# Causal mask of an attention kernel: from mask matmuls before the exponential to GpSimd selects behind it

## The chip, the cores and the metric

One core of a Trainium2 chip. The metric is the device time in microseconds (us) of one execution, the median of several. The profile is of a single execution. Engines: PE (TensorE, matrix products), DVE (VectorE), ACT (ScalarE), POOL (GpSimd), and SP (SyncE), which here only starts DMA transfers. PSUM is the accumulator memory of PE, of 8 banks; SBUF is the working memory.

## What is computed

The kernel computes attention and a gated feed-forward on the same normalised input, for 4 batches of 512 tokens and width 512, 16 heads of 32, hidden width 1408:

```
xn = layernorm(x)
q, k, v = split(xn @ w_qkv)            # 16 heads of 32
q, k = rope(rmsnorm(q)), rope(rmsnorm(k))
scores = q @ k.T / sqrt(32)
scores = where(q_idx >= k_idx, scores, -1e30)
s = (softmax(scores) @ v) @ w_out
g = silu(down(silu(gate(xn)) * up(xn)))
out = x + s * g
```

The mask lets a query see the keys up to its own position.

## The kernel before, in words

Every engine runs a program of its own, written out by hand, and waits on counting semaphores. Values are split into a high and a low part (`_h`, `_l` or `ph`, `pl`), two reduced-precision numbers whose sum is the full one, and products are taken of both.

**Beats.** `run_beats` steps through 73 beats, c = -8 to 64. Beat j works on head j of 64 (4 batches x 4 groups x 4 heads) and at the same time on later heads: PE projects for beat j + 7, POOL and DVE normalise and rotate for j + 6, PE turns q and k for j + 5 (`turn`), and the row maxima of the group after next are found (`maxima`, `max_turn`) and sent by SP into a spare row of `qst` (`m0_out`, `m_out`). Into the gaps PE puts the gate and up products (`gate_half`, 12 of each 16 beats; the other four turn the next batch's input, `xn_turn`) and the output projection (`out_proj`). The order on each engine is that of its `beat` function. After beat 64 comes the down projection (`down`), whose weights and inputs SP starts to load in beat 57 (`LOAD_AT`), 22 transfers in a row.

**A head.** Of the transposed scores (keys down, queries across) only blocks on and below the causal diagonal are computed, in three groups (`ST_OPS`): widths 512; 384 and 128; 256. Each of the four key blocks begins with a 128 x 128 block on the diagonal. `scores_t(r, c, e)` computes group e. In a key block the diagonal part is masked by a second product into the same bank, identity (`idb`) times a table with -1e30 for keys later than the query (`msk_t`), both bf16. `exps` on ACT takes the exponential twice, as f32 `pf` and as reduced `ph`; `p_low` on DVE makes `pl` = `pf` - `ph` and counts `pl_ok`; `p_v(r, c, e)` on PE waits for `pl_ok` and adds `ph` and `pl` times the values. In beat j PE runs the groups 0, 1, 2 of `scores_t`, and `p_v` of group 0 last; groups 1 and 2 of `p_v` follow in beat j + 1, behind groups 0 and 1 of its scores. `exps` of a group waits for `p_v` of the same group of the head before (`pv_ok`).

**POOL** does, in a beat: `inv_rms` (a `pow` of 8 numbers per partition), `rope` (three products), in some beats `rstd_block`, then `out_sum` (where c mod 4 is 1) and `norm` (where it is 2), for a group of four heads that is done. `norm` waits for `rdb`, the reciprocal row sums, which go through DRAM by two DMAs of SP.

Of the kernel before, what the change touches and what calls it, by code (L numbers as in the profile page):

```python
# [7 lines left out]
ALU = mybir.AluOpType  # L8
# [3 lines left out]
F32R = mybir.dt.float32r  # L12
# [3 lines left out]
B, N, H = 4, 512, 512  # L16
# [31 lines left out]
AT_CG, AT_QST, AT_MX = 129152 // 4, 146016 // 4, 195424 // 4  # L48
# [25 lines left out]
def build(nc, x, w_qkv, w_out, q_gamma, k_gamma, w_gu, s_gate, s_up, w_down, s_down,  # L74
          cos_tab, sin_tab, ident, ident_b, mask_s, mask_t, s_dram, rd_dram, wg_dram, hf_dram, out):
    top = ExitStack()
    with top:
# [39 lines left out]
        msk_t = sb("msk_t", [P, P], BF16)  # L117
# [25 lines left out]
        ph = sb("ph", [P, sum(ST_W)], F32R)  # L143
        pl = sb("pl", [P, sum(ST_W)], F32R)
# [48 lines left out]
        st_full, p_ok, pl_ok, pv_ok, o_ev = (sem(n) for n in ("st_full", "p_ok", "pl_ok", "pv_ok", "o_ev"))  # L193
# [87 lines left out]
        def _(sp):  # L281
# [8 lines left out]
            for dst, src in ((ctab, cos_tab), (stab, sin_tab), (gam[:, 0, :], q_gamma.to_broadcast([P, HD])),  # L290
                             (gam[:, 1, :], k_gamma.to_broadcast([P, HD])), (idb[:], ident_b),
                             (msk_s[:], mask_s), (msk_t[:], mask_t)):
                sp.dma_start(dst, src).then_inc(c_in, 16)
# [192 lines left out]
        def _(pool):  # L486
# [7 lines left out]
            def tables():  # L494

                pool.wait_ge(c_in, 16 * 7)
# [34 lines left out]

            def out_sum(i):

                wait(pool, og_in, 16 * 2 * HG * (i + 1))
                wait(pool, onl_ok, i)
                pool.tensor_tensor(on[:], oh[:], ol[:], ALU.add).then_inc(os_ok, 1)
# [6 lines left out]
            def beat(r, c):  # L543
                j, k = 16 * r + c, c % 4
                if there(j + 6, NB):
                    inv_rms(j + 6, (c + 6) % 2)
                if there(j + 6, NB):
                    rope(j + 6, (c + 6) % 2, (c + 6) % 4)
                b, t = ln_at(r, c)
# [6 lines left out]
                if k == 2 and there(4 * r + (c - 6) // 4, B * G):  # L556
                    norm(4 * r + (c - 6) // 4)

# [420 lines left out]
        def _(pe):  # L979
# [46 lines left out]
            def scores_t(r, c, e):  # L1026
# [7 lines left out]
                for j, c0, w in ST_OPS[e]:  # L1034
                    pe.matmul(bank[:, c0:c0 + w], kst[0:KS + 1, par, h, j * P:(j + 1) * P],  # L1035
                              qst[0:KS + 1, par, h, j * P:N], start=True, stop=False)
                    op = pe.matmul(bank[:, c0:c0 + P], idb[:], msk_t[:], start=False, stop=True)  # L1037
                op.then_inc(st_full, 1)

            def p_v(r, c, e):  # L1040

                j_, v, h = 16 * r + c, c // 4 % VR, c % 4
                pe.wait_ge(pl_ok, NOP * j_ + e + 1)
# [91 lines left out]
            def beat(r, c):  # L1135
# [3 lines left out]
                if isinstance(r, int) and r == 0 and c == -4:  # L1139
                    pe.wait_ge(c_in, 16 * 7)  # L1140
# [155 lines left out]
```

## Time and profile before

| | |
|---|---|
| median of 3 runs | 802.47 us (801.33 to 804.57) |
| profiled execution, its own time | 800.7 us |
| its span, first to last instruction | 798.7 us |
| mean granted TensorE clock | 0.967 |
| PE, DVE, ACT, POOL busy | 716.4, 536.0, 450.0, 291.9 us |

The busy times are sums over the span. The end of a PE row is modelled, so the busy share of PE overstates what it does; the distance between starts is the surer measure. A wait in the trace is idle time of an engine that ended when another's result came.

### The profile page before, as it was taken

The numbers are of one execution on the slowest core, as the hardware profiler recorded it, in microseconds if no ns is written. First come the engines' busy times: TensorE is split into PE (matmuls) and PEld (weight loads), VectorE is DVE, ScalarE is ACT, GpSimd is POOL, SyncE is SP. The second block draws the span as 40 slices with busy tenths as digits, with TensorE's granted clock in tenths as the row PEclk, the third lists the DMA queues.
The fourth block names the chain that finished last, engine by engine and source line by source line (L and its number), as shares of the span: only waits on it lengthen the run. The fifth ranks groups of instructions, "written<-read, shape, count | busy, mean of one in ns | idle before, by whom it ended". The sixth has DMA issues, their size and how long they took to land.

```text
span 798.7 us, 12896 instructions
## 1 busy us (share of the span) xinstructions
PE 716.4 (90%) x4160; PEld 575.3 (72%) x4160; DVE 536.0 (67%) x1051; ACT 450.0 (56%) x1007; POOL 291.9 (37%) x338
## 2 busy tenths in 40 slices
PE   2589999889999999899999999899999972798997
PEld 2477877777787887677878877778788751586885
DVE  2677677887767677867676677776764672746373
ACT  1444666577565555766665567766655672634230
POOL 5544335555444434553433445534333330100000
PEclk9699999999999999999999999999999995699999
DMA  8154433412333332123333222033332136278672
GB/s 289 32 170 153 147 127 116 135 54 75 93 106 94 114 103 71 54 68 95 105 94 121 87 74 67 15 94 107 94 118 87 50 117 223 73 253 298 211 251 92
DMA packets 59280, 94.36 MB, mean 118 GB/s; under 512 B 12752, under 2 KB 15440, under 8 KB 59216
## 3 DMA queue, kind: packets, MB, share of 16 engines
q1 hardware_dynamic: 59216, 93.56, 36.9%
q8 instruction: 34, 0.56, 0.3%
q14 instruction: 30, 0.25, 0.1%
HBM read 59.06 MB, written 25.82 MB: 106 GB/s over the span
## 4 chain that ended last, share of the span: by engine, by line
PE 73%; DVE 8%; issue 5%; DMA 5%; SPq 3%; POOL 2%; ACT 2%; DVEq 0%; ACTq 0%; POOLq 0%
PE bank L1115 19%; PE bank L1010 17%; PE bank L1051 8%; PE bank L1131 6%; PE bank L1091 5%; PE bank L1035 5%; PE bank L1072 5%; PE bank L1022 3%; PE bank L1037 2%; PE bank L1074 2%; DVE pl L821 2%; SPq L346 1%; DVE qn L798 1%; DMA rd_dram<-rd 1%; DVE mx L840 1%
## 5 line engine op out<-in xcount | busy, mean ns | idle before, releaser
L840 DVE TENSOR_REDUCE mx<-bank 128x1 f32<-128x384 f32 (+3 forms) x176 | 109.4, 636 | 88.0 <-PE bank L1074 87.2
L517 POOL TENSOR_TENSOR rr<-ss,half 128x8 f32<-128x8 f32 x64 | 106.3, 1661 | 149.1 <-DVE ss L791 149.1
L625 ACT ACTIVATE pf<-bank 128x512 f32<-128x512 f32 (+1 forms) x192 | 101.0, 526 | 101.5 <-PE bank L1037 68.9
L821 DVE TENSOR_TENSOR pl<-pf,ph 128x512 fp32r<-128x512 f32 (+1 forms) x192 | 132.0, 688 | 15.6 <-ACT ph L626 15.1
L523 POOL TENSOR_TENSOR ra<-qn,cg 128x256 f32<-128x256 f32 x64 | 47.0, 734 | 153.3 <-DVE qn L798 153.3
L1115 PE MATMUL bank<-xnt_h,wgu 128*128 128x512 f32 x352 | 98.7, 402 | 3.7 <-DVE g L867 1.6
L626 ACT ACTIVATE ph<-bank 128x512 fp32r<-128x512 f32 (+1 forms) x192 | 101.2, 527 | 0.0
L1115 PE MATMUL bank<-xnt_l,wgu 128*128 128x512 f32 x352 | 96.3, 395 | 0.0
L1035 PE MATMUL bank<-qst,kst 97*128 97x512 f32 (+3 forms) x256 | 81.8, 373 | 13.9 <-DMA qst<-mrow 13.5
L1072 PE MATMUL bank<-kst,qst 96*128 96x128 f32 (+3 forms) x256 | 83.7, 378 | 1.3 <-DVE mx L840 1.3
L1051 PE MATMUL bank<-ph,va 128*65 128x512 f32 (+3 forms) x256 | 76.9, 326 | 4.9 <-ACT oraw L634 3.0
L526 POOL TENSOR_TENSOR rb<-qn,sg 128x128 f32<-128x128 f32 x128 | 79.4, 640 | 0.0
L1115 PEld LDWEIGHTS bank<-xnt_l,wgu 128*128 128x128 f32 x352 | 66.1, 188 | 16.3
L1010 PE MATMUL bank<-wq_h,xnt_h 128*128 128x384 f32 x256 | 62.0, 365 | 17.3 <-DVE va L802 15.7
L614 ACT ACTIVATE kst<-bank 96x512 fp32r<-96x512 f32 x64 | 38.1, 595 | 60.5 <-PE bank L1022 59.5
L1010 PE MATMUL bank<-wq_h,xnt_l 128*128 128x384 f32 x256 | 72.0, 365 | 0.0
L1051 PE MATMUL bank<-pl,va 128*65 128x512 f32 (+3 forms) x256 | 71.9, 317 | 0.0
L1131 PE MATMUL bank<-wd,ht_h 128*128 128x512 f32 x176 | 70.7, 402 | 1.2 <-DVE wd L883 0.8
L1115 PEld LDWEIGHTS bank<-xnt_h,wgu 128*128 128x128 f32 x352 | 60.8, 188 | 14.5 <-issue 4.9
L1131 PE MATMUL bank<-wd,ht_l 128*128 128x512 f32 x176 | 70.3, 400 | 0.0
L1035 PEld LDWEIGHTS bank<-qst,kst 97*128 97x128 f32 x256 | 51.3, 200 | 22.0 <-DMA qst<-mrow 14.3
L1022 PE MATMUL bank<-idr,tt 128*96 128x128 f32 x512 | 55.7, 232 | 10.0 <-DVE xnt_l L785 6.0
(84 smaller groups left out, 1400.6 us busy)
## 6 DMA issues: line engine op xcount, KB each, us to landing
wgu<-wg_dram SPq DMA_DIRECT2D x66, 256.0 KB, 2.8
hf_dram<-g SPq DMA_DIRECT2D x44, 256.0 KB, 3.0
hf_raw<-hf_dram SPq DMA_DIRECT2D x44, 256.0 KB, 6.0
wg_dram<-wgu SPq DMA_DIRECT2D x22, 256.0 KB, 3.1
xr<-x SPq DMA_DIRECT2D x16, 256.0 KB, 3.4
stage<-w_gu SPq DMA_DIRECT2D x16, 256.0 KB, 3.4
oh<-oraw SPq DMA_DIRECT2D x64, 64.0 KB, 1.9
ol<-oraw SPq DMA_DIRECT2D x64, 64.0 KB, 2.0
```

Source lines behind the costliest of these rows:

```text
L517: pool.tensor_tensor(rr[:, s, :], ss[:, s, :], half[:], ALU.pow).then_inc(rr_ok, 1)
L625: act.activation(pf[:, tile], bank[:, 0:w], ACT.Exp, scale=SCALE)
L626: act.activation(ph[:, tile], bank[:, 0:w], ACT.Exp, scale=SCALE).then_inc(p_ok, 1)
L821: dve.tensor_tensor(pl[:, tile], pf[:, tile], ph[:, tile].bitcast(F32), ALU.subtract).then_inc(pl_ok, 1)
L840: dve.tensor_reduce(mx[:].rearrange("p (h t) -> p h t", t=TB)[:, h0:h0 + len(heads), qb], bank[:, 0:len(heads) * w].rearrange("p (h n) -> ...
L1010: op = pe.matmul(QKV_PS[:, 0:3 * GC], x_[:, k, t * P:(t + 1) * P], w_[:, k, cols], start=(a == 0), stop=(a == len(todo) - 1))
L1022: op = pe.transpose(W_PS[0:KS, h * P:(h + 1) * P].bitcast(F32R), tt[:, s, h, 3 * a:3 * a + 3, :].rearrange("p c d -> p (c d)"), idr[:])
L1035: pe.matmul(bank[:, c0:c0 + w], kst[0:KS + 1, par, h, j * P:(j + 1) * P], qst[0:KS + 1, par, h, j * P:N], start=True, stop=False)
L1051: op = pe.matmul(PV_PS[0:VW, j * P:N], va[:, v, j, h, :], part[:, a:a + w], start=(j == 0 and part is ph), stop=(j == 2 and part is pl))
L1072: pe.matmul(bank[:, a * w:(a + 1) * w], qst[0:KS, par, h, qb * P:(qb + 1) * P], kst[0:KS, par, h, 0:w], start=True, stop=False)
L1115: op = pe.matmul(GU_PS[:], wgu[:, s, k, :], x_[:, k, :], start=(a == 0), stop=(a == len(todo) - 1))
L1131: op = pe.matmul(DN_PS[t][:], h_[:, m, t * P:(t + 1) * P], wd[:, m, :], start=(m == 0 and h_ is ht_h[b % 2]), stop=(m == MT - 1 and h_ is ...
```

## The change

The table `msk_t`, its load and the second product of `scores_t` go, so the exponentials above the diagonal are taken of unmasked scores. `ph` and `pl` become halves of one tile `pp`. A new POOL function `keep_past(j, e)` waits for `pl_ok` of the group and, for each of its key blocks, writes zero over the entries above the diagonal in both halves at once (an `affine_select` of 128 partitions x 2 x 128), then counts `tri_ok`. `p_v` waits for `tri_ok` in the place of `pl_ok`. Loads counted by `c_in` are one fewer.

```
-        ph = sb("ph", [P, sum(ST_W)], F32R)
-        pl = sb("pl", [P, sum(ST_W)], F32R)
+        pp = sb("pp", [P, 2, sum(ST_W)], F32R)
+        ph, pl = pp[:, 0], pp[:, 1]
...
+            def keep_past(j, e):
+
+                pool.wait_ge(pl_ok, NOP * j + e + 1)
+                for _, c0, _ in ST_OPS[e]:
+                    a = ST_AT[e] + c0
+                    op = pool.affine_select(pp[:, :, a:a + P], pp[:, :, a:a + P], [[0, 2], [1, P]], ALU.is_ge, 0.0,
+                                            base=0, channel_multiplier=-1)
+                op.then_inc(tri_ok, 1)
...
                     inv_rms(j + 6, (c + 6) % 2)
+                if there(j, NB):
+                    keep_past(j, 0)
                 if there(j + 6, NB):
                     rope(j + 6, (c + 6) % 2, (c + 6) % 4)
+                if there(j, NB):
+                    keep_past(j, 1)
                 b, t = ln_at(r, c)
...
                     norm(4 * r + (c - 6) // 4)
+                if there(j, NB):
+                    keep_past(j, 2)
...
                 for j, c0, w in ST_OPS[e]:
-                    pe.matmul(bank[:, c0:c0 + w], kst[0:KS + 1, par, h, j * P:(j + 1) * P],
-                              qst[0:KS + 1, par, h, j * P:N], start=True, stop=False)
-                    op = pe.matmul(bank[:, c0:c0 + P], idb[:], msk_t[:], start=False, stop=True)
+                    op = pe.matmul(bank[:, c0:c0 + w], kst[0:KS + 1, par, h, j * P:(j + 1) * P],
+                                   qst[0:KS + 1, par, h, j * P:N], start=True, stop=True)
...
-                pe.wait_ge(pl_ok, NOP * j_ + e + 1)
+                pe.wait_ge(tri_ok, NOP * j_ + e + 1)
```

On PE, the first rows of a beat in the middle of the program, before: two groups of scores (L1035, with the mask products L1037), a product for the maxima (L1072) and the first of `p_v` (L1051).

```order
L1035 MATMUL bank<-qst,kst 128x512 [waits p_ok]
L1037 MATMUL bank<-msk_t,idb 128x128
L1035 MATMUL bank<-qst,kst 128x384 [waits p_ok]
L1037 MATMUL bank<-msk_t,idb 128x128
L1035 MATMUL bank<-qst,kst 128x128
L1037 MATMUL bank<-msk_t,idb 128x128
L1072 MATMUL bank<-kst,qst 128x384 [waits sm_ok,tk_ev,tq_ev]
L1074 MATMUL bank<-msk_s,idb 128x128
L1051 MATMUL bank<-ph,va 65x384 [waits pl_ok]
L1051 MATMUL bank<-pl,va 65x384
L1051 MATMUL bank<-ph,va 65x128
L1051 MATMUL bank<-pl,va 65x128
```

The same place in the changed kernel (line numbers shift: L1049 is `scores_t`, L1085 `maxima`, L1064 `p_v`):

```order
L1049 MATMUL bank<-qst,kst 128x512 [waits p_ok]
L1049 MATMUL bank<-qst,kst 128x384 [waits p_ok]
L1049 MATMUL bank<-qst,kst 128x128
L1085 MATMUL bank<-kst,qst 128x384 [waits sm_ok,tk_ev,tq_ev]
L1087 MATMUL bank<-msk_s,idb 128x128
L1064 MATMUL bank<-pp,va 65x384 [waits tri_ok]
L1064 MATMUL bank<-pp,va 65x384
L1064 MATMUL bank<-pp,va 65x128 x2
```

The three mask products are gone, weights of one scores product now follow those of another directly, and `p_v` waits for `tri_ok`.

On POOL, the rows of one beat with `norm` before (`inv_rms` L517, `rope` L523 and L526, `norm` L541), and the first of the next beat:

```order
L517 TENSOR_TENSOR rr<-ss,half 128x8 [waits ss_ok]
L523 TENSOR_TENSOR ra<-qn,cg 128x256 [waits qp_ok,qn_ok]
L526 TENSOR_TENSOR rb<-qn,sg 128x8x16 x2
L541 TENSOR_TENSOR on<-on,rdb 128x512 [waits rb_in,os_ok]
L517 TENSOR_TENSOR rr<-ss,half 128x8 [waits ss_ok]
```

The same beat in the changed kernel (`inv_rms` L516, `rope` L522 and L525, `norm` L549, the selects L536):

```order
L516 TENSOR_TENSOR rr<-ss,half 128x8 [waits ss_ok]
L536 AFFINE_SELECT pp<-pp 128x2x128 [waits pl_ok]
L522 TENSOR_TENSOR ra<-qn,cg 128x256 [waits qp_ok,qn_ok]
L525 TENSOR_TENSOR rb<-qn,sg 128x8x16 x2
L536 AFFINE_SELECT pp<-pp 128x2x128 [waits pl_ok]
L536 AFFINE_SELECT pp<-pp 128x2x128
L549 TENSOR_TENSOR on<-on,rdb 128x512 [waits rb_in,os_ok]
L536 AFFINE_SELECT pp<-pp 128x2x128 [waits pl_ok]
L516 TENSOR_TENSOR rr<-ss,half 128x8 [waits ss_ok]
```

One select now stands ahead of `rope`, two ahead of `norm`, and the last behind `norm`, so it can't start before `norm` has had its DMA.

## Rows read from the trace of the kernel before

**Rows 1.** The page's chain that ended last: shares of the span by engine

```profile
PE 73%; DVE 8%; issue 5%; DMA 5%; SPq 3%; POOL 2%; ACT 2%; DVEq 0%; ACTq 0%; POOLq 0%
```

**Rows 2.** Windows: length, busy us (count) of PE, PEld, DVE, ACT, POOL; PE clock, DMA

```profile
100.00:630.00 530.00, 508.06 (x3131) 410.08 (x3131) 378.12 (x761) 332.31 (x770) 232.43 (x249) 1.00 0.30 90
```

**Rows 3.** PE's waits, 100 to 630, then 600 to 700: total us, times, longest

```profile
PE bank L1010 <- DVE va L802: 12.5, 21, 1.0
PE bank L1022 <- DVE xnt_l L785: 2.2, 9, 0.3
...
PE bank L1035 <- DMA qst<-mrow: 13.5, 1, 13.5
```

**Rows 4.** Timeline of PE: start us, duration us, line, out<-in, form, count

```profile
612.77 0.28 PE L1035 MATMUL bank<-qst,kst 97*128 97x256 f32 x1
...
612.94 1.17 PE L1091 MATMUL bank<-wo_h,on_l 128*128 128x512 f32 x4
613.95 0.86 PE L1010 MATMUL bank<-wq_h,xnt_h 128*128 128x384 f32 x4
...
619.38 0.39 PE L1051 MATMUL bank<-pl,va 128*65 128x512 f32 x1
619.61 0.39 PE L1035 MATMUL bank<-qst,kst 97*128 97x512 f32 x1
...
619.88 0.42 PE L1035 MATMUL bank<-qst,kst 97*128 97x384 f32 x1
...
620.18 0.30 PE L1035 MATMUL bank<-qst,kst 97*128 97x128 f32 x1
...
620.37 0.47 PE L1072 MATMUL bank<-kst,qst 96*128 96x512 f32 x1
...
622.27 0.33 PE L1051 MATMUL bank<-pl,va 128*65 128x384 f32 x1
622.44 0.22 PE L1051 MATMUL bank<-ph,va 128*65 128x128 f32 x1
...
622.56 0.28 PE L1051 MATMUL bank<-ph,va 128*65 128x256 f32 x1
622.68 0.28 PE L1051 MATMUL bank<-pl,va 128*65 128x256 f32 x1
```

**Rows 5.** POOL's instructions by form: count | busy us, mean ns | idle before

```profile
L517 POOL TENSOR_TENSOR rr<-ss,half 128x8 f32<-128x8 f32 x64 | 106.3, 1661 | 149.1 <-DVE ss L791 149.1
...
L523 POOL TENSOR_TENSOR ra<-qn,cg 128x256 f32<-128x256 f32 x64 | 47.0, 734 | 153.3 <-DVE qn L798 153.3
...
L505 POOL TENSOR_SCALAR hsc<-sgu 128x11 f32<-128x11 f32 x1 | 0.3, 255 | 5.8 <-DMA sgu<-s_up 5.8
```

**Rows 6.** Timeline of DVE, POOL and PE in one steady beat

```profile
404.81 0.68 DVE L821 TENSOR_TENSOR pl<-pf,ph 128x512 fp32r<-128x512 f32 x1
...
407.81 1.29 POOL L541 TENSOR_TENSOR on<-on,rdb 128x512 f32<-128x512 f32 x1 [0.33 <-DMA rdb<-rd_dram]
...
407.95 1.70 DVE L821 TENSOR_TENSOR pl<-pf,ph 128x512 fp32r<-128x512 f32 x1
...
411.44 0.41 DVE L821 TENSOR_TENSOR pl<-pf,ph 128x256 fp32r<-128x256 f32 x1
...
414.87 0.29 PE L1051 MATMUL bank<-ph,va 128*65 128x256 f32 x1
```

**Rows 7.** Timeline of POOL and PE where `norm` comes late

```profile
335.55 1.28 POOL L541 TENSOR_TENSOR on<-on,rdb 128x512 f32<-128x512 f32 x1 [2.71 <-DMA rdb<-rd_dram]
...
337.01 0.28 PE L1051 MATMUL bank<-ph,va 128*65 128x256 f32 x1
...
688.66 0.42 PE L1051 MATMUL bank<-ph,va 128*65 128x256 f32 x1
...
690.94 1.28 POOL L541 TENSOR_TENSOR on<-on,rdb 128x512 f32<-128x512 f32 x1 [9.45 <-DMA rdb<-rd_dram]
...
694.03 0.77 PE L1131 MATMUL bank<-wd,ht_h 128*128 128x512 f32 x1 [0.79 <-DVE wd L883]
```

More of the change, by code:

```diff
@@ L47 @@
 RING = 4
-AT_CG, AT_QST, AT_MX = 129152 // 4, 146016 // 4, 195424 // 4
+AT_CG, AT_QST, AT_MX = 128896 // 4, 145760 // 4, 195168 // 4
 HELD_B = AT_CG - 65536 // 4 - MT * N
@@ L74, in build @@
 def build(nc, x, w_qkv, w_out, q_gamma, k_gamma, w_gu, s_gate, s_up, w_down, s_down,
-          cos_tab, sin_tab, ident, ident_b, mask_s, mask_t, s_dram, rd_dram, wg_dram, hf_dram, out):
+          cos_tab, sin_tab, ident, ident_b, mask_s, s_dram, rd_dram, wg_dram, hf_dram, out):
     top = ExitStack()
@@ L116, in build @@
         msk_s = sb("msk_s", [P, P], BF16)
-        msk_t = sb("msk_t", [P, P], BF16)
         gam = sb("gam", [P, 2, HD])
@@ L192, in build @@
         m0_in = sem("m0_in")
-        st_full, p_ok, pl_ok, pv_ok, o_ev = (sem(n) for n in ("st_full", "p_ok", "pl_ok", "pv_ok", "o_ev"))
+        st_full, p_ok, pl_ok, tri_ok, pv_ok, o_ev = (sem(n) for n in ("st_full", "p_ok", "pl_ok", "tri_ok", "pv_ok", "o_ev"))
         og_in, d_in, rd_ok, rd_out, rb_in = (sem(n) for n in ("og_in", "d_in", "rd_ok", "rd_out", "rb_in"))
@@ L291, in _ @@
                              (gam[:, 1, :], k_gamma.to_broadcast([P, HD])), (idb[:], ident_b),
-                             (msk_s[:], mask_s), (msk_t[:], mask_t)):
+                             (msk_s[:], mask_s)):
                 sp.dma_start(dst, src).then_inc(c_in, 16)
@@ L494, in tables @@
             def tables():
-                pool.wait_ge(c_in, 16 * 7)
+                pool.wait_ge(c_in, 16 * 6)
                 for a in range(2):
@@ L1139, in beat @@
                 if isinstance(r, int) and r == 0 and c == -4:
-                    pe.wait_ge(c_in, 16 * 7)
+                    pe.wait_ge(c_in, 16 * 6)
                     pe.wait_ge(ones_ok, 4)
@@ L1280 @@
         "mask_s": np.where(tri[None, :] > tri[:, None], NEG, 0.0).astype(ml_dtypes.bfloat16),
-        "mask_t": np.where(tri[:, None] > tri[None, :], NEG, 0.0).astype(ml_dtypes.bfloat16),
     }
@@ L1292 @@
           d["s_up"], d["w_down"], d["s_down"], d["cos_tab"], d["sin_tab"], d["ident"], d["ident_b"],
-          d["mask_s"], d["mask_t"], s_dram, rd_dram, wg_dram, hf_dram, out)
+          d["mask_s"], s_dram, rd_dram, wg_dram, hf_dram, out)
     r = run_bass_kernel_spmd(nc, [arrays], core_ids=[0])
```

## The prediction

> **What bounds the kernel now.** I read four things in turn. The chain that ended last [rows 1]: 73% of it is TensorE (PE). Then the steady stretch, 100 to 630 us [rows 2]: PE busy 508 of 530 us at full granted clock, VectorE (DVE) 378, GpSimd (POOL) 232. The stretch holds 53 beats (53 `ra` groups on POOL, one for each), so a beat is 10.0 us, with 9.6 us of PE, 7.1 us of DVE and 4.4 us of POOL. Then what PE waits for there [rows 3]: mostly DVE's evacuation of the projection bank, 12.5 us in 21 waits, and the low part of the turned input, 2.2 us in 9. So PE's instruction stream is the bound, and what is taken from it comes off the time, except in the beats with such a wait. Last the end: one wait of 13.5 us for a DMA of the row maxima [rows 3]. That DMA stands in SP's queue behind the 22 loads that SP issues at `LOAD_AT` (beat 57), so what happens in beats 57 to 59 vanishes in that wait, for good or ill.
>
> **What the removed matmuls cost.** Four a beat, 256 in all. A PE row ends by a model, so I go by the distance from start to start [rows 4]. For the first two groups of a beat, with masks: 619.61 to 619.88 is 0.27 us (512 columns and a mask), to 620.18 another 0.30 (384 and a mask), to 620.37 another 0.19 (128 and a mask): 0.76 us. Without a mask the same widths take 0.23 us (512, 619.38 to 619.61), 0.17 (384, 622.27 to 622.44) and 0.06 (128, 622.44 to 622.56 is two of them): 0.46. Saved: 0.30 us. The mask itself shows only 0.04 us from its start to the next; the rest is the next weight load, which a short mask matmul can't cover and a wide one can. For the third group, 256 columns and a mask take 0.17 us (612.77 to 612.94) against 0.12 (622.56 to 622.68), and the four 512-column matmuls behind it take 1.01 us (612.94 to 613.95) against 4 x 0.23 = 0.92 with nothing exposed. Saved: 0.05 + 0.08, that is 0.13. **In all 0.42 us a beat.** The low end is 0.04 x 4 = 0.16, if the weight loads stay exposed for another reason.
>
> Beats 0 to 56 count: 57 x 0.42 = 23.9 us. In the 21 beats that wait for the projection bank, the third group stands between DVE's source and that wait, so its 0.13 us only lengthens the wait: 21 x 0.13 = 2.7 off. The first two groups lie ahead of the PE result on which DVE then waits, and stay saved. That leaves 21.2 us.
>
> **What the selects cost.** Four `affine_select` a beat, each 128 partitions x 256 f32 elements (the high and the low half of one 128-column block), one input. The trace has none. The nearest rows [rows 5]: 734 ns for a two-input product of the same size; 255 ns for a one-input operation of 11 elements, a floor, as it is nearly all start-up. The `pow` at 1661 ns for 8 elements warns that an operation with software of its own can cost far more than its size says; I keep it as the upper end. I take 0.5 us, midway between floor and product, since one input is read and the comparison is simple. Four are 2.0 us, and POOL comes to 6.4 us of a beat of 9.6.
>
> The Trainium skill (GPSIMD Engine Reference, section 4.1 on engine selection) tells to keep elementwise work off GpSimd, where two inputs halve the rate while one input runs near line rate; no select is in this trace to check that on.
>
> **Where the selects lie.** `keep_past(j, 0)` runs between `inv_rms` and `rope`, in the time in which POOL waits for `qn`. The low part that it waits for ends at 404.81 + 0.68 = 405.49 in [rows 6]; its reader `p_v(j, 0)` is the last thing in PE's beat, behind two gate halves and the projection. It is hidden. `keep_past(j, 1)` (two selects) waits for a low part that ended at 409.65, and its reader comes in the next beat just ahead of 414.87: hidden too. `keep_past(j, 2)` follows a low part that ends at 411.85; the reader is the row at 414.87, 3.0 us later, some 2.7 with the masks gone. With 0.5 us it is hidden, if POOL is free. What gives way behind it is `inv_rms`, which fits, since its input is ready only about then.
>
> Two costs remain. First the lock. In [rows 6] a low-part subtraction (two SBUF inputs) that takes 0.68 us took 1.70, because POOL's product had started 0.14 us before it: it ended 0.55 us after POOL did, so it did nothing until then. The skill (SBUF — State Buffer, section on who interferes with whom) says just this: an exclusive lock between a DVE operation with two SBUF inputs and a GpSimd operation that reads SBUF. The trace agrees: 1.02 us lost to a 1.29 us product. So each select can hold DVE's `p_low`, `t_low` and `rope_sum` for up to 0.5 us; if all four did so in every beat, DVE would come to 7.1 + 2.0 = 9.1 us of 9.6, the second rival's case. In ordinary beats DVE has 2.9 us idle and PE waits for it nowhere, so this is free. In the four beats a batch that turn the next batch's input there are no gate matmuls ahead, and PE waits on DVE twice (all 9 waits for the input's low part [rows 3], and my count puts most of the 21 there too): a hold there comes straight through. I price it at two holds of 0.5 us a batch, three batches: 3 us.
>
> Second POOL's own queue. `keep_past(j, 2)` stands behind `norm`, which waits for the `rdb` DMA. Where the gate matmuls fill the beats, `norm` is early: 407.81 + 1.29 = 409.10 against 414.87 [rows 6]. Once a batch, where they are missing, it is not: 335.55 + 1.28 = 336.83 against 337.01 [rows 7]. There PE stalls 0.5 to 1 us, but in these same beats it later waits on DVE for about as much, and that chain starts ahead of the stall; I count 0.5 us for all. At the end it is worse: `norm` of group 14 starts at 690.94 after a long wait, and the third group of head 62 now stands behind it, which PE reached at 688.66 [rows 7]. Its select ends near 692.7, then head 63's last scores, exponentials, low part and select have to follow, and the last weight conversions on DVE behind those, which the down projection at 694.03 waits for. I put that at 2.5 us. The same thing at head 58 falls into the 13.5 us wait.
>
> Sum: 21.2 - 3 - 0.5 - 2.5 = 15.2 us saved; the freed constant DMA at the start is under half a microsecond and left out. Against the profiled execution's own 800.7 us this is 785.5. The median of the runs is 1.8 us above that execution, so the forecast is **787.5 us**, 1.9% faster.
>
> **Rivals.**
> *The masks were nearly free.* The weight loads stay exposed and only the 0.16 us a beat is saved: 57 x 0.16 = 9.1, less 4 to 6 for the costs above: about 798. For it: the model of PE's ends. Against: the start distances are not modelled ends, and all three distances that begin right behind a mask (0.30, 0.19 and the 1.01 of four) hold the same 0.09 more than their columns need. Chance 0.08.
> *DVE is held everywhere.* If the selects delay DVE's chain to the projection bank in ordinary beats too, by the 0.4 us that PE saved, the gain goes into those waits: 57 x 0.42 given back, about 800. Against: only 21 of the 53 beats wait for it now, and of DVE's two-input operations only `t_low` and `p_low(j, 0)` stand ahead of it in a beat, with one select at most beside each. Chance 0.10.
> *Slower: POOL becomes the bound.* POOL has 10.0 - 4.4 = 5.6 us free in a beat of today, so from 1.4 us a select it sets the pace. At the 1.66 us of `pow` a beat takes 4.4 + 6.6 = 11.0 us, 1.0 more than now: 57 us, about 860. For it: POOL's software operations are the least predictable rows here. Against: 256 elements through one input should not cost twice the two-input product. Between 1.0 and 1.4 us latencies pile up (`rope` late, DVE held 4 us a beat) and the time is somewhere between 800 and 810. Chance 0.13 for all of it.
> My forecast (780 to 794) holds 0.69.
>
> **How the numbers follow.** A measurement here tells about 0.5% (4 us) from no change. Faster by more than that: the forecast, the first rival's better half and a part of the second, 0.78. Within 0.5%: 0.09. Slower: 0.13. The range runs from 779 (all 23.9 us saved, nothing paid) to 801 (the second rival); what is left out is the slower case and a little at the bottom.
>
> **What would show it.** In the changed kernel's profile: the start distance from the first to the third scores matmul of a beat down from 0.57 to about 0.40; a select near 0.5 us; POOL busy about 130 us more; 256 fewer matmuls on PE; the waits on DVE's projection evacuation longer by about 0.13 each, not more frequent; new waits of PE on a select in few beats, the longest at heads 58 and 62. The forecast is wrong if a select is over 1 us, if PE waits for selects in ordinary beats, or if the 512-wide low-part subtractions grow to well above 1 us on average and PE's waits on DVE multiply.

## The result, and the profile after

The changed kernel takes 795.62 us (median of 11 runs, 792.33 to 802.14) against 802.47 (11 runs, 800.48 to 804.7): the ratio is 0.9926 with a 95% interval of 0.9899 to 0.9954. It is faster, by 0.7%, where 1.9% was forecast. By the medians 6.9 us are gained, less than half of the 15.2 us forecast. The profiled execution took 794.34 us, its span is 792.2 us. Against the forecast of 787.5 us, 8.1 us of gain are missing.

The page's chain that ended last, shares of the span by engine, and part of its shares by line, answers to [rows 1]:

```profile
PE 63%; DMA 10%; POOL 8%; DVE 7%; issue 6%; SPq 4%; ACT 1%; DVEq 0%; POOLq 0%; ACTq 0%
PE bank L1128 18%; PE bank L1024 15%; PE bank L1064 6%; PE bank L1144 6%; PE bank L1104 5%; PE bank L1085 4%; DMA rdb<-rd_dram 3%; PE bank L1049 3%; PE bank L1036 3%; DMA rd_dram<-rd 2%; POOL rr L516 2%; PE bank L1087 2%; SPq L345 1%; POOL pp L536 1%; DVE pp L835 1%
```

PE gave up ten points of the chain (73 to 63). POOL took six of them, but DMA took five, and the DMAs named are not the big loads: they are `rd_dram<-rd` and `rdb<-rd_dram`, the way of the softmax reciprocals through DRAM to `norm`. That is the first pointer to the cause.

PE's waits over the whole span (total us, times, longest), of which [rows 3] shows the stretches for before:

```profile
PE bank L1064 <- POOL pp L536: 19.3, 11, 4.8
PE bank L1024 <- DVE va L816: 17.7, 25, 2.0
PE bank L1049 <- DMA qst<-mrow: 9.3, 1, 9.3
PE bank L1036 <- DVE xnt_l L799: 6.0, 8, 1.6
```

Then two rows of the page's costliest groups: the select, which no earlier row priced (x instructions, busy us, mean ns, idle before), and DVE's low part:

```profile
L536 POOL TENSOR_SCALAR_AFFINE_SELECT pp<-pp 128x256 fp32r<-128x256 f32 x256 | 109.5, 440 | 159.2 <-DVE pp L835 159.2
...
L835 DVE TENSOR_TENSOR pp<-pf,pp 128x512 fp32r<-128x512 f32 (+1 forms) x192 | 127.1, 663 | 15.2 <-ACT pp L640 14.4
```

A select takes 0.44 us, and the low part did not get longer on average (688 ns before, 663 now). That mean mixes two forms: taken apart, the low part of 512 columns fell from 813 to 697 ns and that of 256 columns rose from 436 to 594, so selects do hold DVE, but elsewhere less is held. The price of a select is not the miss; what the lock has to do with it comes below. The 19.3 us of waits on a select fall in 11 places: the longest are 2.8 us between the first scores of heads 27 and 28 and, in the last beats, 4.8 and 3.9.

**Where along the run.** I took the start of the first 512-column scores matmul of each head from PE's timeline, and from those starts the length of each beat, in both kernels. Over heads 0 to 57 the time fell from 570.6 to 558.2 us, so 12.4, where the sum had 17.7 (21.2 less 3 and 0.5). In 48 of these 57 beats the difference is even: -0.40 us on average, 19.3 us in all. The missing part sits in the other nine, those that end at heads 7, 8, 11, 12, 27, 28, 43, 44 and 45: together they are 6.9 us **longer** than before, and one of them, from head 27 to 28, has 2.9 of it.

These are rows of that beat and of the one before it, on POOL, PE, DVE and SP's queue, in the changed kernel (start us, duration us, what it is; in brackets the idle time before it and what ended it):

```profile
319.29 0.24 DVE L861 RECIPROCAL rd<-den 128x16 f32<-128x16 f32 x1
320.07 0.95 POOL L536 TENSOR_SCALAR_AFFINE_SELECT pp<-pp 128x256 fp32r<-128x256 f32 x2
320.98 1.46 POOL L544 TENSOR_TENSOR on<-oh,ol 128x512 f32<-128x512 f32 x1
322.51 0.53 SPq L355 DMA_DIRECT2D oh<-oraw  x1
323.73 0.57 SPq L367 DMA_DIRECT2D rd_dram<-rd  x1
326.89 0.60 SPq L375 DMA_DIRECT2D rdb<-rd_dram  x1
330.51 0.66 PE L1064 MATMUL bank<-pp,va 128*65 128x384 f32 x4
332.31 1.26 POOL L549 TENSOR_TENSOR on<-on,rdb 128x512 f32<-128x512 f32 x1 [4.43 <-DMA rdb<-rd_dram]
333.53 0.41 POOL L536 TENSOR_SCALAR_AFFINE_SELECT pp<-pp 128x256 fp32r<-128x256 f32 x1
333.90 1.64 POOL L516 TENSOR_TENSOR rr<-ss,half 128x8 f32<-128x8 f32 x1
333.99 0.45 PE L1064 MATMUL bank<-pp,va 128*65 128x256 f32 x2 [2.82 <-POOL pp L536]
336.74 1.62 PE L1024 MATMUL bank<-wq_h,xnt_h 128*128 128x384 f32 x4 [0.24 <-DVE va L816]
```

Read it from the top. The two selects of group 1 stand ahead of `out_sum` (L544). It ends at 322.44. The reciprocals have been ready since 319.53, but in SP's queue their store stands behind the next group's gathers into `oh` and `ol`, which may not overwrite what `out_sum` still reads: so `out_sum` releases the gathers (322.51), and behind them the reciprocals go out (323.73) and back (326.89). `norm` (L549) starts at 332.31, after POOL has waited 4.43 us. PE had ended group 1's `p_v` at 331.17 and waits 2.82 us for a select of 0.41 us that stands behind `norm`. The next row of PE that matters, the projection at 336.74, takes 1.62 us for four matmuls that take 0.94 at 318.32 in the same trace. The windows say why (length, busy us and count of PE, PEld, DVE, ACT, POOL, then the granted clock):

```profile
330.00:335.00 5.00, 2.04 (x13) 1.23 (x12) 1.99 (x5) 2.88 (x6) 2.69 (x3) 1.00 0.09 33
335.00:340.00 5.00, 4.24 (x18) 3.57 (x19) 3.20 (x7) 1.21 (x4) 3.66 (x7) 0.51 0.11 28
340.00:345.00 5.00, 4.94 (x30) 4.19 (x30) 2.46 (x7) 3.44 (x10) 2.05 (x2) 0.81 0.11 30
```

PE is busy 2.04 of 5 us around the stall, and right after it the granted clock is 0.51, which is the lower of the two levels, 1.2 GHz. So the stall is paid for a second time. But the kernel before has a low clock in this beat too, with the same row:

```profile
340.38 1.62 PE L1010 MATMUL bank<-wq_h,xnt_h 128*128 128x384 f32 x4 [0.49 <-DVE va L802]
```

From there to the first scores of head 28 it takes 4.83 us (340.38 to 345.21) and the changed kernel 5.68 (336.74 to 342.42). Of the 2.9 us between the two kernels in this beat, about 0.85 are therefore the longer stretch at the low clock, and the rest is mainly the stall itself.

### The profile page after: what moved, and what is told of

Same layout as the page of the kernel before. It is cut to its first block, busy times and chain, and to the rows that moved or that the text cites. A ratio compares the mean times of both kernels' runs of the same rounds, so it can differ in the third digit from the quotient of the medians.

```text
span 792.2 us, 12640 instructions
## 1 busy us (share of the span) xinstructions
PE 699.1 (88%) x3904; PEld 576.4 (73%) x3904; DVE 537.5 (68%) x1051; ACT 449.3 (57%) x1007; POOL 399.8 (50%) x594
## 4 chain that ended last, share of the span: by engine, by line
PE 63%; DMA 10%; POOL 8%; DVE 7%; issue 6%; SPq 4%; ACT 1%; DVEq 0%; POOLq 0%; ACTq 0%
PE bank L1128 18%; PE bank L1024 15%; PE bank L1064 6%; PE bank L1144 6%; PE bank L1104 5%; PE bank L1085 4%; DMA rdb<-rd_dram 3%; PE bank L1049 3%; PE bank L1036 3%; DMA rd_dram<-rd 2%; POOL rr L516 2%; PE bank L1087 2%; SPq L345 1%; POOL pp L536 1%; DVE pp L835 1%
## 5 line engine op out<-in xcount | busy, mean ns | idle before, releaser
L536 POOL TENSOR_SCALAR_AFFINE_SELECT pp<-pp 128x256 fp32r<-128x256 f32 x256 | 109.5, 440 | 159.2 <-DVE pp L835 159.2
L835 DVE TENSOR_TENSOR pp<-pf,pp 128x512 fp32r<-128x512 f32 (+1 forms) x192 | 127.1, 663 | 15.2 <-ACT pp L640 14.4
L516 POOL TENSOR_TENSOR rr<-ss,half 128x8 f32<-128x8 f32 x64 | 107.5, 1680 | 53.6 <-DVE ss L805 53.6
L1064 PE MATMUL bank<-pp,va 128*65 128x512 f32 (+3 forms) x512 | 105.9, 328 | 22.7 <-POOL pp L536 19.3
L640 ACT ACTIVATE pp<-bank 128x512 fp32r<-128x512 f32 (+1 forms) x192 | 100.9, 526 | 0.0
L1064 PEld LDWEIGHTS bank<-pp,va 128*65 128x65 f32 x512 | 59.0, 144 | 39.5 <-POOL pp L536 23.6
L1085 PE MATMUL bank<-kst,qst 96*128 96x128 f32 (+3 forms) x256 | 82.7, 375 | 0.0
L1024 PE MATMUL bank<-wq_h,xnt_h 128*128 128x384 f32 x256 | 60.9, 362 | 19.3 <-DVE va L816 17.7
L1049 PE MATMUL bank<-qst,kst 97*128 97x512 f32 (+3 forms) x256 | 68.1, 341 | 9.3 <-DMA qst<-mrow 9.3
L1024 PE MATMUL bank<-wq_h,xnt_l 128*128 128x384 f32 x256 | 74.0, 373 | 0.0
L525 POOL TENSOR_TENSOR rb<-qn,sg 128x128 f32<-128x128 f32 x128 | 72.7, 588 | 0.0
L1128 PEld LDWEIGHTS bank<-xnt_h,wgu 128*128 128x128 f32 x352 | 61.1, 188 | 11.6 <-issue 2.7
L1049 PEld LDWEIGHTS bank<-qst,kst 97*128 97x128 f32 x256 | 50.5, 201 | 21.9 <-DMA qst<-mrow 10.1
```

The source lines that it names most:

```text
L516: pool.tensor_tensor(rr[:, s, :], ss[:, s, :], half[:], ALU.pow).then_inc(rr_ok, 1)
L536: op = pool.affine_select(pp[:, :, a:a + P], pp[:, :, a:a + P], [[0, 2], [1, P]], ALU.is_ge, 0.0, base=0, channel_multiplier=-1)
L640: act.activation(ph[:, tile], bank[:, 0:w], ACT.Exp, scale=SCALE).then_inc(p_ok, 1)
L835: dve.tensor_tensor(pl[:, tile], pf[:, tile], ph[:, tile].bitcast(F32), ALU.subtract).then_inc(pl_ok, 1)
L1024: op = pe.matmul(QKV_PS[:, 0:3 * GC], x_[:, k, t * P:(t + 1) * P], w_[:, k, cols], start=(a == 0), stop=(a == len(todo) - 1))
L1049: op = pe.matmul(bank[:, c0:c0 + w], kst[0:KS + 1, par, h, j * P:(j + 1) * P], qst[0:KS + 1, par, h, j * P:N], start=True, stop=True)
```

## The experiments

Each ratio is to the kernel before, run beside it on the same chip; it is worked out from all runs of both, so it can differ by 0.1 to 0.3 points from that of the medians. The column "to head 57" is the stretch from head 0 to head 57 in the one execution that was profiled, which need not be the median one (e2's took 788.44 us, e5's 789.27).

| kernel | median us | ratio, 95% interval | to head 57 |
|---|---|---|---|
| before | 801.3 to 803.1 | 1 | 570.6 |
| changed kernel | 795.62 | 0.9926, 0.9899 to 0.9954 | 558.2 |
| e1 select of group 2 first | 796.42 | 0.9916, 0.9882 to 0.9949 | 560.9 |
| e2 no selects | 785.74 | 0.9788, 0.9756 to 0.982 | 551.6 |
| e3 masks and selects | 811.05 | 1.0097, 1.0062 to 1.0131 | 572.9 |
| e4 both moves | 788.52 | 0.9817, 0.9789 to 0.9846 | 553.3 |
| e5 matmul mask for group 2 | 792.11 | 0.9879, 0.9847 to 0.9911 | 554.9 |
| e6 `out_sum` moved alone | 792.77 | 0.9862, 0.9824 to 0.9899 | 556.7 |
| e7 wider selects, on e4 | 793.60 | 0.9889, 0.9854 to 0.9923 | 559.1 |
| e8 group 2's select moved alone | 792.69 | 0.9877, 0.9845 to 0.991 | 555.0 |
| e9 e4, `norm` a beat later | 784.49 | 0.9774, 0.9747 to 0.9802 | 549.6 |
| e10 `norm` a beat later, alone | 784.87 | 0.9788, 0.9759 to 0.9817 | 551.3 |
| e11 before, `norm` a beat later | 800.96 | 0.9976, 0.9956 to 0.9995 | 569.5 |

**First: is it the place in GpSimd's queue, or are selects costly wherever they stand?** The theory (Q) was the queue: `keep_past(j, 2)` behind `norm`. The rival (L) was the lock on DVE and the selects' own latency.

e1 puts the select of group 2 ahead of `out_sum` and `norm`.

```diff
                 b, t = ln_at(r, c)
                 if t is not None:
                     rstd_block(b, t)
...
+                if there(j, NB):
+                    keep_past(j, 2)
                 if k == 1 and there(4 * r + (c - 5) // 4, B * G):
                     out_sum(4 * r + (c - 5) // 4)
                 if k == 2 and there(4 * r + (c - 6) // 4, B * G):
                     norm(4 * r + (c - 6) // 4)
-                if there(j, NB):
-                    keep_past(j, 2)
```

> The third select group of a beat, keep_past(j, 2), stands ahead of out_sum and norm on GpSimd instead of behind them. All else is the changed kernel. Theory Q (queue): what is missing from the forecast was lost because this select waited behind norm, and norm for its DMA. Then TensorE's waits for a select between 100 and 630 us (6.9 us in 5) fall to under 1 us, the lumps of 1 to 3 us at heads 7, 8, 12, 28, 44 and 45 shrink, and the time falls by 6 to 9 us to about 787. Theory L (lock): it was lost because selects hold VectorE's two-input operations. The selects are as many and as long, so the time stays within 2 us of 795.6.

Measured 796.42: no gain, which is the result that theory L was given. Yet in its trace PE waits for no select between 100 and 610 us. What PE waits for there instead:

```profile
PE bank L1024 <- DVE va L816: 17.4, 21, 2.3
PE bank L1036 <- DVE xnt_l L799: 3.9, 9, 0.8
```

Against 12.5 and 2.2 before [rows 3]. Four beats, those that end at heads 8, 11, 12 and 44, are 1.8 to 2.5 us longer than before. In the one from head 11 to 12 `norm` starts 0.11 us ahead of DVE's `t_low` (L829), an operation with two SBUF inputs, which then takes 1.45 us instead of 0.42:

```profile
177.68 1.28 POOL L549 TENSOR_TENSOR on<-on,rdb 128x512 f32<-128x512 f32 x1 [0.96 <-DMA rdb<-rd_dram]
177.79 1.45 DVE L829 TENSOR_TENSOR tt<-qp,tt 128x256 fp32r<-128x256 f32 x1 [0.35 <-ACT tt L616]
```

PE waits 0.63, 0.23 and 0.21 us for DVE behind it, and the granted clock is 0.72 in the window from 180 to 185. One beat earlier `out_sum` (167.91) does the same to `t_low` (168.38, 1.09 us). So the order of POOL's queue also decides which DVE operation `norm` and `out_sum` collide with. The theory, "one select is in the wrong place", was too narrow.

e2 leaves out the selects (and so the causal mask of the diagonal blocks); e3 has the mask matmuls and the selects.

```diff
-                if there(j, NB):
-                    keep_past(j, 0)
...
-                pe.wait_ge(tri_ok, NOP * j_ + e + 1)
+                pe.wait_ge(pl_ok, NOP * j_ + e + 1)
```

> No mask matmuls and no selects: p_v waits for pl_ok, and entries above the diagonal of the diagonal blocks stay in the probabilities (the causal mask is left out there). This is the whole gain of the removed matmuls with no cost of the selects. By the forecast's first term: 57 beats x 0.42 us less the 2.7 us that goes into existing waits, so 21 us below the kernel before, about 781. If the mask matmuls had been worth only their own 0.04 us each, it would be about 794. Both Q and L expect the first; what lies between this run and the changed kernel is what the selects cost.

> The changed kernel with the mask matmuls put back beside the selects, so masked twice: the kernel before plus the selects. Price of the selects at the old pace of TensorE. Q: slower than the kernel before by 5 to 9 us (the late norms of heads 10, 26, 42 and the tail), with the stalls 0.3 to 0.6 us shorter each than in the changed kernel, since the beats are longer. L: also slower by that, but spread over the beats: VectorE's waits grow and each ordinary beat is 0.1 us or more longer.

e2 measured 785.74 where about 781 was expected. To head 57 it saves 19.0 us, a tenth less than the 21.2 forecast; over the whole program it saves 17 us; in its profiled execution the part behind the first down projection is 4.0 us longer than before, which is left open. e3 measured 811.05, 8 us above the kernel before, as expected under Q. By e2 and the changed kernel the selects cost 10 to 11 us, by e3 and the kernel before 8: the loss belongs to the selects, with the masks or without. Theory L expected e3's ordinary beats to be 0.1 us longer each; the 48 even ones differ from the kernel before by 0.02 us on average, and the beats that end at heads 12 and 44 by 2.5 and 1.1.

e4 has both moves: `out_sum` ahead of group 1's selects, the select of group 2 ahead of `norm`.

```diff
+                if k == 1 and there(4 * r + (c - 5) // 4, B * G):
+                    out_sum(4 * r + (c - 5) // 4)
                 if there(j, NB):
                     keep_past(j, 1)
...
-                if k == 1 and there(4 * r + (c - 5) // 4, B * G):
-                    out_sum(4 * r + (c - 5) // 4)
+                if there(j, NB):
+                    keep_past(j, 2)
                 if k == 2 and there(4 * r + (c - 6) // 4, B * G):
                     norm(4 * r + (c - 6) // 4)
-                if there(j, NB):
-                    keep_past(j, 2)
```

> As e1, and out_sum stands ahead of keep_past(j, 1) as well, so that SyncE's gathers and the DMAs of the reciprocal sums behind them start as early as in the kernel before. Q: as e1 or up to 2 us faster, about 786, since norm's DMA lands about 1 us earlier. L: no change from the changed kernel, 795. If e4 is slower than e1, the price is keep_past(j, 1) behind out_sum's own wait for its gathers.

Measured 788.52: 7 us come back with all 256 selects in place. What selects cost wherever they stand can then be little more than the 2.8 us left to e2. L falls for the main part. e4 and e1 differ only in the place of `out_sum`, so in e1 that place alone cost 8 us.

**Second: which of the two moves?** e6 has only the first piece of that diff, e8 only the second.

> Only out_sum moves, ahead of the select of group 1; the select of group 2 stays behind norm. If the loss comes by the chain out_sum, its gather, the reciprocals' way through DRAM, norm, the select of group 2, then a sum that is ready a select earlier (about 0.5 to 1 us) takes that much from each late norm: 792 to 794 us. If only the place of the select of group 2 behind norm counts, nothing changes against the changed kernel: 795 to 797 us.

> Only the select of group 2 moves, to just ahead of norm; out_sum keeps its place between the selects of groups 1 and 2. If the place behind norm is what costs, this is as fast as the kernel with both moves, 788 to 790 us. If out_sum's delay by the select of group 1 counts by itself (it holds back the reciprocals and VectorE), 791 to 793 us.

792.77 and 792.69. Against the changed kernel's 0.9926 the ratios are lower by 0.0064 and 0.0049; together that is 0.0113, and e4, with both, is lower by 0.0109. So both count, and they add up as far as intervals of 0.3 to 0.4 points to either side can tell. For e8 that was the second branch of its expectation; its trace shows what is late when the select no longer is:

```profile
331.28 1.45 POOL L549 TENSOR_TENSOR on<-on,rdb 128x512 f32<-128x512 f32 x1 [3.60 <-DMA rdb<-rd_dram]
332.69 1.63 POOL L516 TENSOR_TENSOR rr<-ss,half 128x8 f32<-128x8 f32 x1
334.36 0.43 DVE L812 TENSOR_TENSOR qn<-bank,rr 128x256 f32<-128x256 f32 x1 [2.76 <-POOL rr L516]
334.70 0.28 DVE L816 TENSOR_TENSOR va<-bank,va 128x128 fp32r<-128x128 f32 x1
335.13 1.62 PE L1024 MATMUL bank<-wq_h,xnt_h 128*128 128x384 f32 x4 [3.41 <-DVE va L816]
```

The wait has moved, not gone: `norm` holds POOL's queue until the DMA lands, behind it now stands the next head's `rr`, DVE waits 2.76 us for that, and PE 3.41 us for DVE. What is wrong is that `norm` is reached before its DMA is in, whatever stands behind it.

e5 gives group 2 its mask by matmul again, so that no select stands behind `norm`, and keeps the other selects (`p_v` of group 2 waits for `pl_ok` again). The edit, against the changed kernel:

```diff
-                    op = pe.matmul(bank[:, c0:c0 + w], kst[0:KS + 1, par, h, j * P:(j + 1) * P],
-                                   qst[0:KS + 1, par, h, j * P:N], start=True, stop=True)
+                    op = pe.matmul(bank[:, c0:c0 + w], kst[0:KS + 1, par, h, j * P:(j + 1) * P],
+                                   qst[0:KS + 1, par, h, j * P:N], start=True, stop=e < 2)
+                    if e == 2:
+                        op = pe.matmul(bank[:, c0:c0 + P], idb[:], msk_t[:], start=False, stop=True)
...
-                if there(j, NB):
-                    keep_past(j, 2)
```

> Group 2 of each head gets its mask from a matmul as before and its p_v waits for VectorE's low part again; groups 0 and 1 keep the selects, and no select stands behind the reciprocal's multiplication. By the theory that the loss of the change is GpSimd's queue (the select of group 2 behind out_sum and norm), this keeps 0.30 us of a beat, about 17 us less 2 that move into waits, and loses nothing in mid-run: 787 to 790 us. By the rival that each select costs VectorE or TensorE something wherever it stands, half of the selects leave about half of the loss: 791 to 795 us.

Measured 792.11, in the range given to the rival (791 to 795) and 2 us above the queue's. The number alone would speak for the rival, by which each select costs something wherever it stands. The trace does not: an ordinary beat is 0.33 us shorter (forecast for the first two groups: 0.30), so its three selects cost nothing there. What stays is `norm`: POOL's waits for its DMA are 49.8 us in 13 over the span (53.1 in 14 in the changed kernel), and the beats that end at heads 12, 44 and 45 are 0.3 to 1.3 us longer than before. The one that ends at head 45 is 1.3 us longer in e2 as well, which has no select. The profiled execution was the fastest of six, so the trace may show too little.

e7 is e4 with selects of 256 columns for three of the four blocks (columns beyond the block's diagonal pass the condition, so the result stays).

```diff
-                for _, c0, _ in ST_OPS[e]:
-                    a = ST_AT[e] + c0
-                    op = pool.affine_select(pp[:, :, a:a + P], pp[:, :, a:a + P], [[0, 2], [1, P]], ALU.is_ge, 0.0,
+                for _, c0, w in ST_OPS[e]:
+                    a, w = ST_AT[e] + c0, min(w, 2 * P)
+                    op = pool.affine_select(pp[:, :, a:a + w], pp[:, :, a:a + w], [[0, 2], [1, w]], ALU.is_ge, 0.0,
```

> The order of the kernel with both moves (out_sum ahead of the select of group 1, the select of group 2 ahead of norm), but three of the four selects of a head take 256 columns instead of 128; the result is the same. Each should take 0.2 to 0.3 us longer, 0.7 us of a beat on GpSimd. If the selects lie in GpSimd's slack, the time stays within 2 us of 788.5. If they hold VectorE, or if p_v waits for them at once, 0.1 to 0.2 us of a beat come back: 795 to 800 us.

Its selects take, by form:

```profile
L536 POOL TENSOR_SCALAR_AFFINE_SELECT pp<-pp 128x512 fp32r<-128x512 f32 x192 | 123.5, 644 | 158.0 <-DVE pp L835 158.0
L536 POOL TENSOR_SCALAR_AFFINE_SELECT pp<-pp 128x256 fp32r<-128x256 f32 x64 | 33.2, 519 | 0.0
```

Twice the elements take 0.20 us more than the 0.44 of the changed kernel. 793.60 is 5 us over e4, between the two branches. In ordinary beats the wider selects cost nothing (-0.3 to -0.48 us against before, as in e4). The difference sits in a few beats; those that end at heads 11 and 27 are 2.2 us longer each. The one from head 26 to 27 shows the lock: three selects, two of them wide, run on POOL from 320.64 to 322.58, and beside them DVE's low part and its `t_low` take 0.83 and 0.85 us, where e4 has 0.62 and 0.64 (0.42 is the usual time of both). `t_low`, e7 and then e4:

```profile
321.99 0.85 DVE L829 TENSOR_TENSOR tt<-qp,tt 128x256 fp32r<-128x256 f32 x1
320.35 0.64 DVE L829 TENSOR_TENSOR tt<-qp,tt 128x256 fp32r<-128x256 f32 x1
```

PE has waits of 0.31, 0.64 and 0.56 us close to each other where e4 has 0.52 and 0.56, and then the granted clock falls. e7 first, then e4, the same window:

```profile
325.00:330.00 5.00, 4.81 (x21) 4.20 (x22) 3.23 (x7) 1.28 (x5) 3.35 (x7) 0.66 0.27 79
```

```profile
325.00:330.00 5.00, 4.79 (x34) 3.71 (x33) 4.13 (x10) 4.00 (x10) 3.15 (x6) 1.00 0.17 58
```

Both show PE busy 4.8 of 5 us, but e7 gets 21 matmuls through and e4 34. A few tenths of a microsecond of waiting more became over 2 us. So e7 bears out its second branch in mechanism (the selects hold VectorE) and the first in ordinary beats, where nobody waits for what is held.

**Third: the move that takes the DMA off the queue.** e10 changes one place only: `norm` is issued in the following beat, behind group 1's selects. e9 does the same to e4. e11 does it in the kernel before, behind `rope`.

```diff
                 if there(j, NB):
                     keep_past(j, 1)
+                if k == 3 and there(4 * r + (c - 7) // 4, B * G):
+                    norm(4 * r + (c - 7) // 4)
...
-                if k == 2 and there(4 * r + (c - 6) // 4, B * G):
-                    norm(4 * r + (c - 6) // 4)
```

> The changed kernel with that one move alone: norm a beat later; out_sum keeps its place behind the select of group 1. If out_sum's delay costs only through the norm that comes late by it, this one move gives the whole 7 us back: 786 to 790 us. If out_sum's later place costs by itself (it holds VectorE or the select of group 2), 791 to 794 us.

> The kernel with both moves, and norm a beat later (in the beats where k is 3, behind the select of group 1), when the DMA that brings the reciprocals should have landed in every case. If the loss of the change is work queued on GpSimd behind a norm that waits for that DMA (a select of group 2, or the next head's rr and through it VectorE's qn and va), the last of it goes: 785 to 788 us, at the level of the kernel without selects. If what is left between them is VectorE held or the extra wait for the select, nothing moves: 788 to 790 us.

> The kernel before, masks by matmul and no selects, with norm a beat later, behind the rotary products. If the late norms cost only because selects stand in GpSimd's queue, nothing changes: 801 to 803 us. If the next head's rr behind a norm that waits for its DMA cost the kernel before something too, the same move is worth 1 to 4 us here: 798 to 801 us.

e10 measured 784.87, 11 us under the changed kernel and at e2's level, with every select in place; e9 784.49; both lie a little under the ranges expected. e11 measured 800.96, in the range of its second branch. POOL's waits over the span, e10:

```profile
POOL pp L536 <- DVE pp L835: 188.5, 126, 15.8
...
POOL on L549 <- DMA rdb<-rd_dram: 15.7, 1, 15.7
```

and the same line of the changed kernel:

```profile
POOL on L549 <- DMA rdb<-rd_dram: 53.1, 14, 15.2
```

The one wait left is the last `norm`, behind all attention work. The beat from head 27 to 28 in e10, where the changed kernel stalled 2.82 us:

```profile
331.46 0.90 PE L1064 MATMUL bank<-pp,va 128*65 128x384 f32 x6
334.08 0.41 POOL L536 TENSOR_SCALAR_AFFINE_SELECT pp<-pp 128x256 fp32r<-128x256 f32 x1 [1.90 <-DVE pp L835]
337.16 1.45 POOL L549 TENSOR_TENSOR on<-on,rdb 128x512 f32<-128x512 f32 x1
```

All six matmuls of groups 1 and 2 run in one piece, `norm` starts without a wait. `out_sum` is as late as in the changed kernel; in this beat that costs nothing, and here its effect in e6 was that of an earlier DMA. Elsewhere it does cost. In e10's trace the beat from head 7 to 8 is 3.4 us longer than before: DVE waits 2.53 us for a load of gate and up weights, its gate product stands behind that, PE waits 2.04 us for the product, and the granted clock is 0.54 in the window from 145 to 150.

```profile
139.54 0.43 DVE L892 TENSOR_SCALAR wgu<-stage 128x512 fp32r<-128x512 int32 x1 [2.53 <-DMA stage<-w_gu]
```

Such loads stand in SP's queue behind the gathers that `out_sum` releases and behind the store of the reciprocals: two are issued at 133.04 and 134.01, in e9, where `out_sum` stands earlier, at 127.87 and 129.79, and there DVE does not wait and the beat is 1.3 us shorter than before. (The kernel before and the changed kernel have DVE wait 1.64 and 2.10 us for this load.) e9 still gains nothing on e10 that can be told (the intervals overlap): over the 48 even beats it takes 3.2 us more, all in the six that end at heads 14, 18, 30, 34, 46 and 50. Why an early `out_sum` costs there was not followed.

e11 gains 0.24% (0.05 to 0.44%): the late `norm` cost the kernel before something too. Its expectation put that down to the next head's `rr` behind `norm`, and the trace shows another way. `rr` ends at 338.62 and DVE reads it only at 339.63. But `norm` started at 335.55 [rows 7], 0.01 us ahead of `t_low`, which was held (0.43 us in e11):

```profile
335.56 1.56 DVE L815 TENSOR_TENSOR tt<-qp,tt 128x256 fp32r<-128x256 f32 x1 [0.35 <-ACT tt L602]
```

The maxima behind it came late, PE waited 0.46 us for them, which it does not in e11, and then the clock was low. First the kernel before, then e11:

```profile
340.00:345.00 5.00, 4.62 (x21) 4.06 (x22) 2.79 (x7) 1.51 (x5) 2.05 (x3) 0.66 0.11 26
```

```profile
340.00:345.00 5.00, 4.51 (x31) 3.73 (x30) 4.01 (x8) 2.93 (x10) 3.56 (x5) 1.00 0.11 26
```

e11's beat is 2.1 us shorter for it, but its next one is 1.5 us longer, at a granted clock of 0.77 from 350 to 355 where the kernel before has 1.00.

## Why the prediction was wrong

Direction and mechanism of the gain were right, the size was not: 6.9 us where 15 were forecast. By its own steps:

**The removed matmuls: right, a little high.** 0.42 us a beat forecast, 0.40 measured over the 48 even beats (0.41 in e10, but 0.37 in e2, which has no selects), and 0.33 for the first two groups alone (e5) against 0.30. (The third group's 0.08 is 0.09 by its own rows, 1.01 less 0.92.) Reading PE by start distances [rows 4] held; by those rows the mask's cost is mostly the exposed weight load behind it.

**The select's price: right.** 0.44 us against 0.5, well inside its bounds [rows 5]. POOL rose by 108 us, where 130 were forecast. The rival in which POOL sets the pace did not occur; nor did free masks, nor DVE held everywhere.

**The lock: the term was too high, and it looked in one place only.** 3 us were put down for selects that hold DVE. They do hold it: the low part of 256 columns takes 594 ns, and 750 in e10, instead of 436. But where they do, PE is seldom waiting. With `norm` late in both kernels the change is worth 15.1 us by the ratio of e10 to e11, 16.1 by their medians; without any select (e2) 17.0 and 17.4. So all selects together cost 1 to 2 us, which is within the error of these runs. A kernel with neither selects nor an early `norm` was not run. What the prediction left out is that POOL's own products hold DVE, and that selects in the queue shift them against DVE's program: `norm` and `out_sum` on `t_low` cost e1 about 2 us in each of two beats, `norm` on `t_low` the kernel before about as much in one. In e10 `norm` falls on a low part (256 columns, 1.51 us at 337.39) for which nobody waits.

**POOL's queue: the step that failed.** It says of the late `norm` once a batch that PE stalls 0.5 to 1 us, "but in these same beats it later waits on DVE for about as much, and that chain starts ahead of the stall; I count 0.5 us for all". With the 2.5 us for the end, POOL's queue was put at 3 us. Measured are about 11 us (795.62 less 784.87, e10) for the whole of `norm`'s place in the queue, of which the kernel before had about 2 already (e11), so some 9 came with the change. Three things are wrong in the step.

First, it compared the old `norm` with an old reader, while the change moves both. The same beat in the kernel before, beside [rows 7]:

```profile
325.76 1.28 POOL L536 TENSOR_TENSOR on<-oh,ol 128x512 f32<-128x512 f32 x1
328.34 0.57 SPq L368 DMA_DIRECT2D rd_dram<-rd  x1
330.02 0.60 SPq L376 DMA_DIRECT2D rdb<-rd_dram  x1
...
336.51 0.37 PE L1051 MATMUL bank<-ph,va 128*65 128x384 f32 x1
```

From the start of `out_sum` to that of `norm` it was 335.55 - 325.76 = 9.79 us; it is 332.31 - 320.98 = 11.33 now, 1.54 more. Nearly all of that is the store of the reciprocals, which SP waits for before it fetches them: 3.16 us from issue to issue (323.73 to 326.89) against 1.68. It takes 1.7 us in most groups of every kernel here and up to 3.8 in some (the last group aside, which takes 4.9 to 6.5); which other transfer it meets then wasn't tried. PE, with its masks gone and `out_sum` a select later, is now nearer: from `out_sum`'s start to group 1's `p_v` it is 330.51 - 320.98 = 9.53 us against 10.75, so 1.22 less. With the select's 0.41 that is 3.17 us; the slack was 337.01 - 336.83 = 0.18 [rows 7]. The rest, 2.99, is the stall: group 2 follows group 1 by 3.48 us (330.51 to 333.99) instead of 0.50. The prediction never followed the way from `out_sum` by SP's queue and two transfers to `norm`.

Second, the stall is hardly taken back by the later waits on DVE. In the rest of the beat PE waited 1.41 us for DVE before and waits 0.90 now, so 0.5 of 2.82 us comes back. `rr` is behind the select and `norm` in the same queue, so DVE's chain moves with the stall; e8 shows it with the select out of the way.

Third, the granted clock. The forecast priced time on PE at full clock throughout. After the stall it was 0.51, and the projection's four matmuls took 1.62 us instead of 0.94. Against the kernel before, which has a low clock here too, that is 0.85 us; against e10, which has 1.00 in all windows from 325 to 345, the stall of 2.82 us makes this beat 5.3 us longer. e7 shows the same with short waits.

Also, it counted the case once a batch. In the trace `norm` waits for its DMA in 11 of the first 13 head groups, 0.7 to 4.4 us each and 28 us in all (before: in 9, 11.6 us), and PE waits 1.1 to 1.2 us for a select in the beats that end at heads 12 and 44 as well. (So it does in the one that ends at head 7, but that wait stays in e10 and is not `norm`'s.)

**The end: too low.** From the first scores of head 60 to head 63 and from there to the down projection the changed kernel takes 15.76 + 9.82 = 25.6 us against 14.65 + 6.76 = 21.4, so 4.2 us more where 2.5 were put down. The wait named is there: group 2 of head 62 waits behind `norm` of group 14,

```profile
682.22 1.26 POOL L549 TENSOR_TENSOR on<-on,rdb 128x512 f32<-128x512 f32 x1 [3.97 <-DMA rdb<-rd_dram]
683.43 1.49 POOL L536 TENSOR_SCALAR_AFFINE_SELECT pp<-pp 128x256 fp32r<-128x256 f32 x4
683.89 0.69 PE L1064 MATMUL bank<-pp,va 128*65 128x256 f32 x2 [3.85 <-POOL pp L536]
```

and four selects of two heads have piled up behind it. With `norm` a beat later (e10) the same stretch costs 15.74 + 7.6 - 21.4 = 1.9 us. The wait forecast at head 58 is there as well, 4.8 us, and as forecast the wait for `qst<-mrow` gives most of it back (9.3 us instead of 13.5).

**The check on the whole.** The profiled executions are 6.5 us apart where the sum had 15.2. Of the 8.7 missing, 5.3 are lost by head 57 (17.7 less 12.4) and 1.7 at the end (4.2 less 2.5); the start and the beats from 57 to 60 are 1.1 us longer each, and the part behind the first down projection is 0.4 shorter. With `norm` out of the way in both kernels the change is worth 800.96 - 784.87 = 16.1 us (e11, e10), near the 15.2 of the sum. That is partly luck: the sum holds 3 us for the queue, which no longer stalls there, and 3 us of lock that these runs do not show, against 21.2 for the masks where e2 gives 17.

**Left open.** The beats from 57 to 60, where the wait for `qst<-mrow` was forecast to swallow all changes, differ by -0.5 to 2.4 us; the start differs by -1.1 to 2.1 us from run to run. Both are unexplained. In e2, e4 and e7 the stretch behind the first down projection takes 2.4 to 4.0 us more than before, in e10 0.5; this wasn't followed either.

## What to carry to other kernels

When an operation is put into a queue that also holds one that waits for a DMA, follow that DMA back to what starts it: the new work delays the start of the transfer as well as the work behind its landing, and a reader that got faster meets both. Price the stall at the clock that comes after it, not at the clock before. The cheapest repair is often not to reorder the new work but to move the waiting instruction to where its data is surely in: here one moved call took the gain from 7 to 18 us by the medians (0.7% to 2.1%). Then look at what the moved instruction now runs beside: a DVE operation that POOL holds up cost nothing here where nobody waited for it, and about 2 us of a beat where PE did.

## What the runs showed of the hardware

The select: 128 partitions x 256 f32 elements in 0.44 us, x 512 in 0.64 (e7), against 0.73 for the two-input product of 256 [rows 5]; by these two, 256 elements more cost 0.2 us, so about half of the short one is start-up, an estimate.

POOL holds up DVE's operations with two SBUF inputs: a `t_low` of 0.42 us took 1.56 and 1.45 us when a POOL product of 1.28 us had started 0.01 and 0.11 us before it, and 0.85 us beside selects of 0.64 us (e7). Whether that costs time depends on who waits: all 256 selects together cost about 1 to 2 us, within the error of these runs.

The two levels of the granted clock came at a low price in waiting: after 2.82 us of stall in one piece (0.51 in the next window), but also after 0.31, 0.64 and 0.56 us spread over one beat with PE busy in between (0.66). Kernels that differ by 0.4 us in such waits (e7 and e4) differed by 2.2 us in the beat.
